# Second attention of a two-layer model: key-row scores from a second matmul, with the row maxima subtracted inside it

## Chip, core and metric

The kernel runs on one core of one Trainium2 chip. The metric is device time in microseconds (us). A profiled execution of the same program gives the trace; its span runs from the first to the last instruction.

## What is computed

1024 tokens of width 512 (2 sequences of 512) pass through an attention, a gated feed-forward, a second attention and a routed low-rank layer; each is added to its input and normalized. The change lies in the second attention (32 query heads, 8 key/value heads, head size 16, so 4 query heads share a key head):

```
q, k = rope(x @ Wq), rope(x @ Wk);  v = x @ Wv
scores = q @ k.T / sqrt(16), causal mask
ctx = softmax(scores) @ v
out = x + ctx @ Wo, normalized
```

## The kernel before

Everything is written by hand for the five engines, with semaphores; each engine runs its list in order. Matrix products are made from high and low parts (three matmuls for one).

The second attention (`attention1`, line 1248) first projects 8 tiles of 128 tokens to queries, keys and values, rotates them (`rotate` on VectorE, `turn_rows` on GpSimd), and turns them so that head elements lie on partitions (`turn_part` on TensorE, `high_part` on ScalarE, `low_part` on VectorE).

Then it works in 16 *units* (2 sequences x 8 key heads) of 4 query heads, 64 *slots* `s` in all. For a unit SyncE copies with 12 DMAs (`load_stacks`, lines 1411 to 1429) the high and low parts of keys and queries into `k_stack` and `q_stack`, 96 rows, so that one matmul with 96 rows gives the full product; keys of head versions 0 and 1 stand in separate rows with zeros between. There are two stacks of each. SyncE waits before load `u` until the scores of unit `u - 2` are made (line 1440).

One slot, over four engines:

- `scores(s)` on TensorE (1867 to 1885): for each of 4 query tiles a matmul, queries x seen keys, 512, 384, 128 and 256 keys wide, into three PSUM banks `ps_s`; a bank is filled again when its maxima are taken.
- `maxima(s)` on VectorE (1653 to 1663): adds the mask, takes the row maximum, writes the masked scores (`a_probs`) and the maximum (`a_neg_max`).
- `exps(s)` on ScalarE (1473 to 1478): four exponentials with the maximum as bias.
- `turn(s)` on TensorE (1887 to 1900): ten 128x128 transposes of probabilities into three banks `ps_t`, so that keys lie on partitions.
- `copy_turned(s)`: VectorE copies the first bank to SBUF (1665 to 1669), ScalarE the two others (1480 to 1486): `f_pT`, a ring of 6 slots.
- once per unit, `apply` (1902 to 1925): values x turned probabilities, four heads in four column strips of the array, in two parts; a column of ones beside the values gives the row sums. `evacuate` on VectorE, `turn_output` on TensorE, `join` on VectorE (division by the sum) follow.

The order is a loop over slots in each engine's list: TensorE does `turn(s)`, a part of `apply` or `turn_output` of the unit before, and `scores(s + 3)`; VectorE `maxima(s + 2)` and `copy_turned(s)`; ScalarE `exps(s + 1)` and `copy_turned(s)`. SyncE's queue carries the stack loads and, between them, weights of later stages; GpSimd splits those weights. After the loop the output is turned in tiles of 128 tokens (`turn_out`, `high_out`, `low_out`) and multiplied with `Wo` (`project_out`), with normalization and the routed layer behind it.

Of the kernel before, what the change touches and what calls it, by code (L numbers as in the profile page):

```python
# [15 lines left out]
P = 128  # L16
# [1184 lines left out]
HIGHEST = 3e38  # L1201
# [3 lines left out]
PROBS_AT = {3: 0, 2: SEQ, 0: SEQ + 3 * P, 1: 2 * SEQ}  # L1205
ROW_TILES = (3, 2, 0, 1)
PIECES = 3


TURNED_AT = {0: (0, 0), 1: (1, 0), 3: (1, 3 * P), 2: (2, 0)}  # L1210
TURNED_WIDTH = (SEQ, SEQ, 2 * P)
KEY_TILES = (0, 1, 3, 2)
# [4 lines left out]
RING = 6  # L1217
VALUE_COLS = HD1 + 2
HEAD_ROWS = P // GROUP1
APPLY_KEYS = ((0, 3), (1, 2))  # L1220
# [3 lines left out]
AHEAD_SCORES, AHEAD_MAXIMA, AHEAD_EXPS = 3, 2, 1  # L1224
CONSTANTS = 3
# [4 lines left out]
PARTS_IN_LOOP = {0: 7, 1: 8, 2: 9}  # L1230
# [17 lines left out]
def attention1(nc, t, w_o, w_f1, lora_b_in, small_in, result, psum):  # L1248

    ctx = ExitStack()  # L1250
    with ctx:
# [17 lines left out]
        q_stack = sb("q_stack", [P, 2, 2, SEQ], F32R)  # L1269
        k_stack = sb("k_stack", [P, 2, 2, SEQ], F32R)  # L1270
# [19 lines left out]
        probs = sb("probs", [P, GROUP1, HEAD_PROBS])  # L1290

        pT = over("pT", [P, RING, HEAD_PROBS], xT_at)
        b_at = aligned(nc.sbuf_base)
        sb("b_place", [P, 2, D])
        oT_now = sb("oT_now", [P, SEQ])
        by_at = aligned(nc.sbuf_base)
        by_cos, by_sin = sb("by_cos", [P, D + KV1 * HD1]), sb("by_sin", [P, D + KV1 * HD1])
        neg_max = sb("neg_max", [P, GROUP1, SEQ_TILES])
# [6 lines left out]
        main_first = over("main_first", [P, 1, D], xT_at + 4 * RING * HEAD_PROBS)  # L1305
# [5 lines left out]
        small = sb("small", [P, sum(SMALL.values())])  # L1311
        low = sb("low", [P, TILES, LORA])
        h = sb("h", [P, TILES, GATE_H])
        hT = sb("hT", [P, 2, P])

# [31 lines left out]
        ps_s, ps_t, ps_o = psum[0:3], psum[3:6], psum[6:8]  # L1347
        ps_out, ps_y, ps_side = psum[0:2], psum[2:4], psum[6:8]
# [6 lines left out]
        pads_set = sem("pads_set")  # L1355
# [5 lines left out]
        scored, max_done, exp_done = sem("scored"), sem("max_done"), sem("exp_done")  # L1361
        pT_ready, pT_dve, pT_act = sem("pT_ready"), sem("pT_dve"), sem("pT_act")
# [33 lines left out]
        def row_probs(s, qt):  # L1396
            return probs[:, s % GROUP1, PROBS_AT[qt]:PROBS_AT[qt] + (qt + 1) * P]

# [7 lines left out]
        def _(sp):  # L1406
# [4 lines left out]
            def load_keys(u, version, arrived):  # L1411
                b, g = divmod(u, KV1)
                for part, source in enumerate((kT_hi, kT_lo, kT_hi)):
                    to = part * PAIR_ROWS + version * HD1
                    sp.dma_start(k_stack[to:to + HD1, u % 2, version, :].bitcast(F32),
                                 source[g * HD1:(g + 1) * HD1, b * SEQ:(b + 1) * SEQ].bitcast(F32)).then_inc(arrived, 16)

            def load_queries(u, pair, arrived):
                b, g = divmod(u, KV1)
                first = (g % 2) * GROUP_COLS + pair * PAIR_ROWS  # L1420
                for part, source in enumerate((qT_hi, qT_hi, qT_lo)):
                    sp.dma_start(q_stack[part * PAIR_ROWS:(part + 1) * PAIR_ROWS, u % 2, pair, :].bitcast(F32),
                                 source[first:first + PAIR_ROWS, g // 2, b * SEQ:(b + 1) * SEQ].bitcast(F32)).then_inc(arrived, 16)
# [9 lines left out]
            sp.wait_ge(pads_set, 1)  # L1433
# [25 lines left out]
        def _(act):  # L1459
# [13 lines left out]
            def exps(s):  # L1473
                h = s % GROUP1
                for qt in ROW_TILES:
                    act.wait_ge(max_done, SEQ_TILES * s + maxima_before(qt))
                    act.activation(row_probs(s, qt), row_probs(s, qt), ACT.Exp, bias=neg_max[:, h, qt:qt + 1],  # L1477
                                   scale=-1.0).then_inc(exp_done, 1)

            def copy_turned(s):  # L1480
                if s >= RING:
                    act.wait_ge(applied, 2 * ((s - RING) // GROUP1 + 1))
                for piece in (1, 2):
                    width, at = TURNED_WIDTH[piece], piece * SEQ
                    act.wait_ge(pT_ready, PIECES * s + piece + 1)
                    act.activation(pT[:, s % RING, at:at + width], ps_t[piece][:, 0:width], ACT.Copy).then_inc(pT_act, 1)

            for tile in range(TILES - 1):
                if tile < 2:
                    norm.high(act, TILES - 2 + tile)  # L1490
                if tile == 0:
                    act.wait_ge(pads_set, 2)
# [5 lines left out]
                if tile == TILES - 2:  # L1498
                    exps(0)
            for s in range(SLOTS1 + 2):  # L1500
                u, h = divmod(s, GROUP1)
                if s + AHEAD_EXPS < SLOTS1:
                    exps(s + AHEAD_EXPS)
                if s < SLOTS1:
                    copy_turned(s)
                if s == 0:
                    copy_values(TILES - 1)
                    act.wait_ge(v_done, TILES)
                if s in PARTS_IN_LOOP:
                    high_part(PARTS_IN_LOOP[s])  # L1510

            def high_out(tile):
                act.wait_ge(out_turned, tile + 1)
                act.activation(outT_hi[:, :, tile * P:(tile + 1) * P], out_bank(tile), ACT.Copy).then_inc(out_hi, 1)
# [21 lines left out]
            for tile in range(4):  # L1536
                high_out(tile)
# [5 lines left out]
            for tile in range(TILES):  # L1543
# [6 lines left out]
                if tile + 4 < TILES:  # L1550
                    high_out(tile + 4)
# [25 lines left out]
        def _(pool):  # L1577
# [7 lines left out]
            pool.memset(k_stack[:, :, :, :].bitcast(F32), 0.0).then_inc(pads_set, 1)  # L1585
            pool.memset(v_flat[:, :], 1.0).then_inc(pads_set, 1)
            def turn_rows(tile):
# [4 lines left out]
            for tile in range(TILES - 1):  # L1592
                turn_rows(tile)
            def raise_diagonal(k):
# [11 lines left out]

            turn_rows(TILES - 1)
            for s in range(2, SLOTS1):
                pool.wait_ge(pT_dve, s)
# [15 lines left out]
        def _(dve):  # L1625
            ahead.add_row(dve, rows, norm, TILES - 1)
# [26 lines left out]
            def maxima(s):  # L1653

                if s >= GROUP1:
                    dve.wait_ge(pT_ready, PIECES * (s - GROUP1 + 1))
                for qt in ROW_TILES:
# [3 lines left out]
                    dve.tensor_tensor_reduce(row_probs(s, qt), ps_s[bank][:, at:at + seen], mask[:, SEQ - seen:SEQ],  # L1661
                                             -SCALE1, HIGHEST, ALU.add, ALU.min,
                                             neg_max[:, s % GROUP1, qt:qt + 1]).then_inc(max_done, 1)

            def copy_turned(s):
                if s >= RING:
                    dve.wait_ge(applied, 2 * ((s - RING) // GROUP1 + 1))
                dve.wait_ge(pT_ready, PIECES * s + 1)
                dve.tensor_copy(pT[:, s % RING, 0:SEQ], ps_t[0][:, :]).then_inc(pT_dve, 1)  # L1669

            def evacuate(n):
                dve.wait_ge(applied, 2 * (n + 1))
                if n >= 1:
                    dve.wait_ge(o_turned, n)
                dve.tensor_copy(oT_now[:, :], ps_o[n % 2][:, :]).then_inc(o_read, 1)
# [23 lines left out]
            for s in range(SLOTS1 + 3):  # L1699
                if s % GROUP1 == 2 and s >= GROUP1:  # L1700
                    evacuate(s // GROUP1 - 1)
                if s + AHEAD_MAXIMA < SLOTS1:
                    maxima(s + AHEAD_MAXIMA)
                if s < SLOTS1:
                    copy_turned(s)
                if s in PARTS_IN_LOOP:
                    low_part(PARTS_IN_LOOP[s])
                if s % GROUP1 == 3 and GROUP1 <= s < SLOTS1:
                    join(s // GROUP1 - 1)
# [13 lines left out]

            def low_out(tile):
                at = slice(tile * P, (tile + 1) * P)
                dve.wait_ge(out_hi, tile + 1)
                dve.tensor_tensor(outT_lo[:, :, at], out_bank(tile), outT_hi[:, :, at].bitcast(F32),
                                  ALU.subtract).then_inc(out_lo, 1)
# [55 lines left out]
            low_out(0)  # L1784
            join(UNITS1 - 1)
            for tile in range(1, 4):
                low_out(tile)
            dve.wait_ge(main_in, 48)
            for tile in range(TILES):
                add_output(tile)  # L1790
                if tile >= 2:
# [3 lines left out]
                if tile + 4 < TILES:  # L1795
                    low_out(tile + 4)
# [51 lines left out]
        def _(pe):  # L1848
# [18 lines left out]
            def scores(s):  # L1867

                u, h = divmod(s, GROUP1)
                if s == 0:  # L1870
                    pe.wait_ge(first_stack_in, STACK_DMAS // 2)
                elif s == 1:
                    pe.wait_ge(stack_in[0], STACK_DMAS // 2)
                elif h == 0:
                    pe.wait_ge(stack_in[u % 2], (u // 2 + 1) * STACK_DMAS - (STACK_DMAS // 2 if u % 2 == 0 else 0))
                for piece, tiles in enumerate(((3,), (2, 0), (1,))):
# [272 lines left out]
```

## Time and profile before

| | |
|---|---|
| median of 3 runs | 1177.17 us (1176.73 to 1177.77) |
| span of the profiled execution | 1175.2 us |
| second attention's loop over 64 slots | about 910 to 1092 us of the span |
| first matmul of the output projection behind it | 1098.4 us |

The span is read stage by stage. In a row of a timeline stand the start, the duration, engine and line, operation, output <- input, and in brackets the idle time before it with what ended it; several like instructions are one row (x4). TensorE has two rows: PE for matmuls (their ends are modelled and overlap) and PEld for weight loads. SPq is SyncE's queue of DMA issues.

### The profile page before, as it was taken

The numbers are of one execution on the slowest core, as the hardware profiler recorded it, in microseconds if no ns is written. First come the engines' busy times: TensorE is split into PE (matmuls) and PEld (weight loads), VectorE is DVE, ScalarE is ACT, GpSimd is POOL, SyncE is SP. The second block draws the span as 40 slices with busy tenths as digits, with TensorE's granted clock in tenths as the row PEclk, the third lists the DMA queues.
The fourth block names the chain that finished last, engine by engine and source line by source line (L and its number), as shares of the span: only waits on it lengthen the run. The fifth ranks groups of instructions, "written<-read, shape, count | busy, mean of one in ns | idle before, by whom it ended". The sixth has DMA issues, their size and how long they took to land. (4 is left out here: it accounts for less than half of the span.)

```text
span 1175.2 us, 20479 instructions
## 1 busy us (share of the span) xinstructions
PE 1135.8 (97%) x6634; PEld 952.6 (81%) x6634; DVE 780.6 (66%) x2463; ACT 705.3 (60%) x1646; POOL 410.5 (35%) x342
## 2 busy tenths in 40 slices
PE   7899999999999999999999999999999899999997
PEld 6788888788888888888888778888888677777786
DVE  6866776667776667766677762223336899999775
ACT  6656665556665566666566544543112899999524
POOL 4654554255444445534443513334013210020200
PEclk9999999999999999999999999999999999999999
DMA  6011110111110100110100012222001223321001
GB/s 230 19 40 43 37 32 24 30 28 37 53 29 21 37 32 24 55 27 11 45 19 28 1 37 75 68 78 76 1 18 24 57 70 80 98 53 33 2 1 72
DMA packets 30364, 51.24 MB, mean 44 GB/s; under 512 B 5680, under 2 KB 6576, under 8 KB 30256
## 3 DMA queue, kind: packets, MB, share of 16 engines
q1 hardware_dynamic: 29680, 48.85, 14.7%
q8 instruction: 55, 0.90, 0.3%
q10 hardware_dynamic: 576, 1.05, 0.2%
q14 instruction: 53, 0.43, 0.1%
HBM read 38.35 MB, written 2.10 MB: 34 GB/s over the span
## 5 line engine op out<-in xcount | busy, mean ns | idle before, releaser
L487 POOL TENSOR_TENSOR turned<-turned,sin 128x512 f32<-128x512 f32 x73 | 94.4, 1293 | 310.3 <-ACT turned L347 310.3
L363 ACT ACTIVATE probs<-probs,neg_max 128x256 f32<-128x256 f32 (+1 forms) x256 | 119.8, 473 | 11.3 <-DVE neg_max L580 11.3
L1477 ACT ACTIVATE a_probs<-a_probs,a_neg_max 128x512 f32<-128x512 f32 (+3 forms) x256 | 122.6, 562 | 0.1
L1661 DVE CUSTOM_DVE_ANT_0 a_probs<-bank,a_mask 128x512 f32<-128x512 f32 (+3 forms) x256 | 109.8, 486 | 6.2 <-PE bank L1881 6.1
L490 POOL TENSOR_TENSOR turned<-turned,by_cos 128x512 f32<-128x512 f32 x73 | 101.1, 1385 | 5.7
L96 PE MATMUL bank<-wo_hi,oT_hi 128*128 128x512 f32 x256 | 100.3, 392 | 1.7 <-DVE oT_lo L643 1.7
L734 PE MATMUL bank<-xT_hi,wq_hi 128*128 128x512 f32 x256 | 101.7, 397 | 0.0
L734 PE MATMUL bank<-xT_lo,wq_hi 128*128 128x512 f32 x256 | 100.3, 392 | 0.0
L734 PE MATMUL bank<-xT_hi,wq_lo 128*128 128x512 f32 x256 | 100.0, 391 | 0.0
L96 PE MATMUL bank<-wo_hi,oT_lo 128*128 128x512 f32 x256 | 99.9, 390 | 0.0
L96 PE MATMUL bank<-wo_lo,oT_hi 128*128 128x512 f32 x256 | 99.7, 389 | 0.0
L426 ACT ACTIVATE oT_hi<-bank 128x512 fp32r<-128x512 f32 x64 | 38.2, 596 | 93.4 <-PE bank L96 93.4
L422 ACT ACTIVATE pT_hi<-bank 128x512 fp32r<-128x512 f32 x112 | 61.6, 595 | 52.0 <-PE bank L773 52.0
L638 DVE TENSOR_TENSOR pT_lo<-bank,pT_hi 128x512 fp32r<-128x512 f32 x112 | 72.8, 686 | 22.1 <-ACT pT_hi L422 16.5
L1899 PE MATMUL bank<-identity,a_probs 128*128 128x128 f32 x640 | 81.3, 274 | 5.0 <-DVE f_pT L1669 5.0
L576 DVE CUSTOM_DVE_ANT_0 probs<-bank,mask 128x256 f32<-128x256 f32 (+1 forms) x256 | 85.0, 386 | 0.0
L553 DVE TENSOR_TENSOR by_cos<-bank,cos 128x512 f32<-128x512 f32 x73 | 50.3, 689 | 49.4 <-ACT turned L347 49.3
L346 ACT ACTIVATE turned<-bank 64x512 f32<-64x512 f32 x73 | 43.5, 596 | 63.3 <-PE bank L734 62.7
L1899 PEld LDWEIGHTS bank<-identity,a_probs 128*128 128x128 f32 x640 | 70.0, 140 | 9.0 <-issue 7.6
L643 DVE TENSOR_TENSOR oT_lo<-bank,oT_hi 128x512 fp32r<-128x512 f32 x64 | 44.2, 691 | 48.9 <-ACT oT_hi L426 47.7
L762 PE MATMUL bank<-kT_hi,qT_hi 128*128 128x256 f32 (+1 forms) x256 | 76.0, 297 | 0.0
L592 DVE TENSOR_SCALAR probs<-probs,inv_sum 128x256 f32<-128x256 f32 (+1 forms) x240 | 72.0, 363 | 2.1
(234 smaller groups left out, 3155.1 us busy)
## 6 DMA issues: line engine op xcount, KB each, us to landing
staged<-weights SPq DMA_DIRECT2D x70, 256.0 KB, 2.7
f_staged<-weights_f SPq DMA_DIRECT2D x33, 256.0 KB, 2.7
a_q_stack<-a_qT_hi SPq DMA_DIRECT2D x64, 64.0 KB, 2.0
rows<-x_rows SPq DMA_DIRECT2D x2, 1024.0 KB, 7.4
a_k_stack<-a_kT_hi SPq DMA_DIRECT2D x64, 32.0 KB, 2.0
a_q_stack<-a_qT_lo SPq DMA_DIRECT2D x32, 64.0 KB, 2.0
out<-rows SPq DMA_DIRECT2D x8, 256.0 KB, 2.0
a_raw<-weights_qkv SPq DMA_DIRECT2D x4, 384.0 KB, 4.4
```

Of the source, the lines that this page charges most:

```text
L96: mm = pe.matmul(out, a, b, start=(n == 0), stop=(n == len(steps) - 1))
L363: act.activation(probs[:, s % 2, h, 0:width], probs[:, s % 2, h, 0:width], ACT.Exp, bias=neg_max[:, s % 2, h:h + 1], scale=SCALE0, accum_o ...
L487: pool.tensor_tensor(at, at, sin[:, :], ALU.mult).then_inc(sin_done, 1)
L490: pool.tensor_tensor(at, at, by_cos_at(a, first), ALU.add).then_inc(roped, 1)
L576: dve.tensor_tensor_reduce(probs[:, s % 2, h, 0:width], ps_s[h // 2][:, (h % 2) * 2 * P:(h % 2) * 2 * P + width], seen, 1.0, LOWEST, ALU.a ...
L592: dve.tensor_scalar(probs[:, s % 2, h, 0:width], probs[:, s % 2, h, 0:width], inv_sum[:, s % 2, h:h + 1], None, ALU.mult).then_inc(probs_d ...
L638: dve.tensor_tensor(pT_lo[:, kb, :], ps_t[kb][:, :], pT_hi[:, kb, :].bitcast(F32), ALU.subtract).then_inc(pT_lo_done, 1)
L734: mm = pe.matmul(ps_a[a % 2][:, :], w[hi][:, k, :], part[:, k, cols], start=(n == 0), stop=(n == 3 * KC - 1))
L762: mm = pe.matmul(ps_s[pair][:, (h % 2) * 2 * P:((h % 2) * 2 + count) * P], q[:, u % 2, h, at], k[:, u % 2, keys], start=(n == 0), stop=(n ...
L1477: act.activation(row_probs(s, qt), row_probs(s, qt), ACT.Exp, bias=neg_max[:, h, qt:qt + 1], scale=-1.0).then_inc(exp_done, 1)
L1661: dve.tensor_tensor_reduce(row_probs(s, qt), ps_s[bank][:, at:at + seen], mask[:, SEQ - seen:SEQ], -SCALE1, HIGHEST, ALU.add, ALU.min, neg ...
L1899: mm = pe.transpose(ps_t[piece][:, at:at + P], row_probs(s, qt)[:, kb * P:(kb + 1) * P], ident[:, :])
```

## The change

Scores are made twice. As before, query rows x keys, from which now only the maxima are kept: VectorE writes its masked scores as bfloat16 into a tile that nobody reads, and the maxima into columns of `tops`. Once per unit TensorE turns the 16 columns of maxima (`turn_tops`), ScalarE copies them negated into `top_rows` (`copy_tops`), and SyncE writes them with 2 DMAs (`load_tops`) into two spare rows of the query stack; GpSimd has set ones in those rows of the key stack. A second set of matmuls with 98 rows (`key_scores`) then gives keys x queries with the maximum already subtracted. ScalarE takes three exponentials straight from PSUM into `pT` (now a ring of 8), and GpSimd sets the part above the diagonal to zero (`prune`). The transposes and copies of probabilities are gone.

The maxima run 7 slots ahead (LEAD), with 4 stacks. The evacuation of a unit moves from VectorE to ScalarE, values are applied in three parts from one slot later, and the turning of the first four output tiles moves into slots 58 to 61; two units' outputs and the last unit's value matmuls move behind the first tiles of the output projection.

```
...
+STACKS = 4
+TOP_ROW = STACK
+STACK_ROWS = STACK + 2
+LEAD = 7
+RING, RING_IN_X = 8, 6
-APPLY_KEYS = ((0, 3), (1, 2))
+APPLY_KEYS = ((0,), (1,), (3, 2))
+APPLY_PARTS = len(APPLY_KEYS)
+APPLY_LAG = GROUP1 + 1
-AHEAD_SCORES, AHEAD_MAXIMA, AHEAD_EXPS = 3, 2, 1
+OUT_AHEAD = 58
...
```

On SyncE:

```
+            def load_tops(u):
+                sp.wait_ge(top_ready, u + 1)
+                for version in range(2):
+                    rows_of = slice(version * 2 * SEQ_TILES, (version + 1) * 2 * SEQ_TILES)
+                    to = q_stack[u % STACKS][TOP_ROW + version:TOP_ROW + version + 1, :, :].rearrange("a p (t c) -> a (p t) c", c=P)
+                    sp.dma_start(to.bitcast(F32), top_rows[rows_of, :].bitcast(F32)).then_inc(top_in[u % 2], 16)
+
+            sp.wait_ge(stack_set, 2 * STACKS)
             sp.wait_ge(part_lo, TURNS_OF[0])
             load_stacks(0)
             load_stacks(1)
-            for u in range(2, UNITS1):
-                if u == KV1:
-                    sp.wait_ge(part_lo, TURNS_OF[1])
-                sp.wait_ge(scored, PIECES * GROUP1 * (u - 1))
-                load_stacks(u)
+            for u in range(UNITS1):
+                load_tops(u)
+                if u + 2 < UNITS1:
+                    if u + 2 == KV1:
+                        sp.wait_ge(part_lo, TURNS_OF[1])
+                    if u >= 2:
+                        sp.wait_ge(keyed, PIECES * GROUP1 * (u - 1))
+                    load_stacks(u + 2)
...
```

On ScalarE:

```
             def exps(s):
                 if s >= RING:
+                    act.wait_ge(applied, APPLY_PARTS * ((s - RING) // GROUP1 + 1))
+                for piece, width in enumerate(KEY_WIDTH):
+                    act.wait_ge(keyed, PIECES * s + piece + 1)
+                    act.activation(pT(s)[:, piece * SEQ:piece * SEQ + width], ps_t[piece][:, 0:width], ACT.Exp,
+                                   scale=SCALE1).then_inc(exp_done, 1)
+
+            def copy_tops(u):
+                act.wait_ge(top_turned, u + 1)
+                act.activation(top_rows[0:4 * SEQ_TILES, :], ps_top[u][0:4 * SEQ_TILES, 0:P], ACT.Copy,
+                               scale=-1.0).then_inc(top_ready, 1)
...
+            for s in range(SLOTS1):
+                exps(s)
+                if s % GROUP1 == 1 and s + 3 < SLOTS1:
+                    copy_tops((s + 3) // GROUP1)
+                if s % GROUP1 == 3 and s >= GROUP1 + 3:
+                    evacuate((s - GROUP1 - 3) // GROUP1)
+                if OUT_AHEAD <= s < OUT_AHEAD + SEQ_TILES:
+                    high_out(s - OUT_AHEAD)
...
```

On GpSimd:

```
+            def pad_keys(n):
+
+                pool.memset(k_stack[n][:, :, :].bitcast(F32), 0.0).then_inc(stack_set, 1)
+                pool.wait_ge(stack_set, 2 * n + 1)
+                pool.affine_select(k_stack[n][:, :, :], k_stack[n][:, :, :], [[-1, 2], [0, SEQ]], ALU.not_equal, 1.0,
+                                   base=-TOP_ROW, channel_multiplier=1).then_inc(stack_set, 1)
...
             for tile in range(TILES - 1):
                 turn_rows(tile)
+                if tile < STACKS:
+                    pad_keys(tile)
...
+            def prune(s):
+
+                pool.wait_ge(exp_done, PIECES * (s + 1))
+                for first, step in ((0, SEQ), (SEQ + 3 * P, P)):
+                    pair = pT(s)[:, first:first + 2 * step].rearrange("p (a c) -> p a c", a=2)[:, :, 0:P]
+                    pool.affine_select(pair, pair, [[0, 2], [1, P]], ALU.is_ge, 0.0, base=0,
+                                       channel_multiplier=-1).then_inc(pruned, 1)
...
```

On VectorE, per slot:

```
+                    dve.tensor_tensor_reduce(unused[:, UNUSED_AT[qt]:UNUSED_AT[qt] + seen], ps_s[bank][:, at:at + seen], mask[:, SEQ - seen:SEQ],
+                                             1.0, LOWEST, ALU.add, ALU.max, top_column(s, qt)).then_inc(max_done, 1)
...
+            for s in range(SLOTS1):
+                if s % GROUP1 == 1 and s >= 2 * GROUP1 + 1:
+                    join((s - 2 * GROUP1 - 1) // GROUP1)
+                if s + LEAD < SLOTS1:
+                    maxima(s + LEAD)
+                if OUT_AHEAD <= s < OUT_AHEAD + SEQ_TILES:
+                    low_out(s - OUT_AHEAD)
...
```

On TensorE:

```
+            def key_scores(s, piece):
+
+                u, h = divmod(s, GROUP1)
+                if h == 0 and piece == 0:
+                    pe.wait_ge(top_in[u % 2], 32 * (u // 2 + 1))
+                if s >= 1:
+                    pe.wait_ge(exp_done, PIECES * (s - 1) + piece + 1)
+                for kb in KEY_PIECES[piece]:
+                    at = KEYS_AT[kb][1]
+                    mm = pe.matmul(ps_t[piece][:, at:at + SEQ - kb * P],
+                                   k_stack[u % STACKS][0:STACK_ROWS, h % 2, kb * P:(kb + 1) * P],
+                                   q_stack[u % STACKS][0:STACK_ROWS, h // 2, kb * P:SEQ], start=True, stop=True,
+                                   skip_group_check=True)
+                mm.then_inc(keyed, 1)
+
+            def turn_tops(u):
+                pe.wait_ge(max_done, SEQ_TILES * GROUP1 * (u + 1))
...
+                if u >= 3:
+                    pe.wait_ge(finished, u - 2)
+                pe.transpose(ps_top[u][:, 0:P], tops[:, u % 2, :], ident[:, :]).then_inc(top_turned, 1)
...
+            lead(2)
+            lead(3)
+            turn_part(PARTS_LAST[0])
+            lead(4)
+            turn_tops(0)
+            turn_part(PARTS_LAST[1])
+            lead(5)
+            turn_part(PARTS_LAST[2])
+            lead(6)
...
+            for s in range(SLOTS1):
+                for piece in range(PIECES):
+                    if s + LEAD < SLOTS1:
+                        scores(s + LEAD, piece)
+                    key_scores(s, piece)
+                if s % GROUP1 == 1 and s + 3 < SLOTS1:
+                    turn_tops((s + 3) // GROUP1)
+                if s >= APPLY_LAG and (s - APPLY_LAG) % GROUP1 < APPLY_PARTS:
+                    apply((s - APPLY_LAG) // GROUP1, (s - APPLY_LAG) % GROUP1)
+                if s % GROUP1 == 0 and s >= 2 * GROUP1:
+                    turn_output(s // GROUP1 - 2)
+                if s == OUT_AHEAD:
+                    pe.wait_ge(max_done, SEQ_TILES * SLOTS1)
+                if OUT_AHEAD <= s < OUT_AHEAD + SEQ_TILES:
+                    turn_out(s - OUT_AHEAD)
             for tile in range(TILES):
                 project_out(tile)
+                if tile == 0:
+                    turn_output(UNITS1 - 2)
+                    for part in range(APPLY_PARTS):
+                        apply(UNITS1 - 1, part)
+                if tile == 1:
+                    turn_output(UNITS1 - 1)
...
```

The scores keep their wait for the stack: the first of a unit's score matmuls waits until all 12 loads of that unit have landed (line 1875 before, unchanged in the new `scores`).

## Rows read from the trace of the kernel before

**Rows 1.** Windows: busy us (instructions) of each engine, TensorE's clock, DMA share, GB/s.
```profile
950.00:1080.00 130.00, 126.57 (x1090) 95.78 (x1088) 121.76 (x460) 123.08 (x284) 8.61 (x16) 1.00 0.27 67
```

**Rows 2.** Timeline of two heads in the steady loop.
```profile
986.11 0.71 PEld L1881 LDWEIGHTS bank<-a_k_stack,a_q_stack 96*128 96x128 f32 x4 [0.20 <-issue]
986.11 0.91 PE L1881 MATMUL bank<-a_k_stack,a_q_stack 96*128 96x512 f32 x4
986.76 0.69 DVE L1661 CUSTOM_DVE_ANT_0 a_probs<-bank,a_mask 128x512 f32<-128x512 f32 x1 [0.35 <-PE bank L1881]
986.76 1.12 PEld L1899 LDWEIGHTS bank<-identity,a_probs 128*128 128x128 f32 x10
...
987.99 0.87 ACT L1486 ACTIVATE f_pT<-bank 128x512 f32<-128x512 f32 x2
988.04 0.16 PEld L1920 LDWEIGHTS bank<-f_pT,a_v_tok 128*32 128x32 f32 x8 [0.17 <-issue]
...
988.41 0.69 DVE L1669 COPY f_pT<-bank 128x512 f32<-128x512 f32 x1
...
988.75 1.91 ACT L1477 ACTIVATE a_probs<-a_probs,a_neg_max 128x512 f32<-128x512 f32 x4
...
989.26 0.71 PEld L1881 LDWEIGHTS bank<-a_k_stack,a_q_stack 96*128 96x128 f32 x4 [0.41 <-issue]
...
993.49 0.47 PEld L1932 LDWEIGHTS bank<-identity,a_oT_now 128*128 128x128 f32 x4
```

**Rows 3.** Timeline of SyncE's queue: stack loads of three units.
```profile
987.11 0.51 SPq L1415 DMA_DIRECT2D a_k_stack<-a_kT_hi  x1
987.66 0.59 SPq L1415 DMA_DIRECT2D a_k_stack<-a_kT_lo  x1
...
993.98 0.59 SPq L1422 DMA_DIRECT2D a_q_stack<-a_qT_lo  x1
...
999.27 0.82 SPq L1415 DMA_DIRECT2D a_k_stack<-a_kT_hi  x1
...
1009.11 0.51 SPq L1415 DMA_DIRECT2D a_k_stack<-a_kT_hi  x1
```

**Rows 4.** The page's DMA issues: count, KB each, median us from issue to landing.
```profile
a_q_stack<-a_qT_lo SPq DMA_DIRECT2D x32, 64.0 KB, 2.0
```

**Rows 5.** Groups on ScalarE, 800 to 1092 us: count | busy us, mean ns | idle before.
```profile
L1486 ACT ACTIVATE f_pT<-bank 128x256 f32<-128x256 f32 x64 | 24.4, 382 | 0.0
...
L1464 ACT ACTIVATE a_v_tok<-bank 128x128 f32<-128x128 f32 x8 | 2.2, 280 | 21.6 <-DVE a_by_sin L1644 21.5
...
L1060 ACT ACTIVATE f_gated<-bank 128x512 f32<-128x512 f32 x2 | 1.2, 598 | 2.9 <-PE bank L96 2.9
```

**Rows 6.** Groups on GpSimd, 500 to 1092 us.
```profile
L518 POOL TENSOR_SCALAR probs<-probs,inv_sum 128x256 f32<-128x256 f32 x12 | 10.9, 923 | 9.3 <-DVE inv_sum L585 9.3
...
L1602 POOL CAST a_w_hi<-f_side_raw 128x256 fp32r<-128x256 f32 x4 | 1.6, 396 | 89.3 <-DVE f_pT L1669 89.3
```

**Rows 7.** Timeline of GpSimd in the projections of the second attention.
```profile
880.31 0.46 POOL L1590 TENSOR_TENSOR a_k_tok<-a_by_cos,a_by_sin 128x128 f32<-128x128 f32 x1
883.61 1.29 POOL L1589 TENSOR_TENSOR a_q_tok<-a_by_cos,a_by_sin 128x512 f32<-128x512 f32 x1 [2.84 <-DVE a_by_sin L1644]
```

**Rows 8.** Timeline of VectorE: the third head's first maximum.
```profile
914.36 0.68 DVE L1661 CUSTOM_DVE_ANT_0 a_probs<-bank,a_mask 128x512 f32<-128x512 f32 x1
```

**Rows 9.** Timeline of TensorE: first matmul of the output projection.
```profile
1098.38 0.48 PE L96 MATMUL bank<-a_w_hi,a_qT_hi 128*128 128x512 f32 x1
```

**Rows 10.** Timeline of TensorE: two early matmuls, and the last of all.
```profile
11.47 0.63 PE L734 MATMUL bank<-xT_hi,wk_lo 128*128 128x512 f32 x1
11.90 0.63 PE L734 MATMUL bank<-xT_hi,wq_hi 128*128 128x512 f32 x1
...
1169.57 0.40 PE L2018 MATMUL bank<-f_b_hi,f_low_T_lo 128*128 128x512 f32 x1
```

**Rows 11.** Windows: the granted clock (after the five engines) behind the last matmul.
```profile
1173.00:1174.00 1.00, 0.00 (x0) 0.00 (x0) 0.00 (x0) 0.00 (x0) 0.00 (x0) 0.51 1.02 381
```

More of the change, by code:

```diff
@@ L1347, in attention1 @@
         ps_s, ps_t, ps_o = psum[0:3], psum[3:6], psum[6:8]
+        ps_top = [psum[5]] + [ps_o[(u + 1) % 2] for u in range(1, UNITS1)]
         ps_out, ps_y, ps_side = psum[0:2], psum[2:4], psum[6:8]
@@ L1360, in attention1 @@
         stack_in = [sem(f"stack_in{n}") for n in range(2)]
-        scored, max_done, exp_done = sem("scored"), sem("max_done"), sem("exp_done")
-        pT_ready, pT_dve, pT_act = sem("pT_ready"), sem("pT_dve"), sem("pT_act")
+        scored, max_done = sem("scored"), sem("max_done")
+        top_turned, top_ready = sem("top_turned"), sem("top_ready")
+        top_in = [sem(f"top_in{n}") for n in range(2)]
+        keyed, exp_done, pruned = sem("keyed"), sem("exp_done"), sem("pruned")
         applied, o_read, o_turned = sem("applied"), sem("o_read"), sem("o_turned")
@@ L1497, in _ @@
                     act.wait_ge(v_done, SEQ_TILES)
[L1498 to L1514, printed above, removed]
+            copy_values(TILES - 1)
+            act.wait_ge(v_done, TILES)
+            high_part(PARTS_LAST[0])
+            copy_tops(0)
+            high_part(PARTS_LAST[1])
+            high_part(PARTS_LAST[2])
+            for s in range(SLOTS1):
[6 more added lines that the diff above has]
+                    high_out(s - OUT_AHEAD)
             def low_rows(tile):
@@ L1625, in _ @@
         def _(dve):
+            dve.memset(tops[:, :, :], 0.0)
             ahead.add_row(dve, rows, norm, TILES - 1)
@@ L1698, in _, with low_out @@
             rotate(TILES - 1)
[L1699 to L1709, printed above, removed]
+            maxima(2)
+            maxima(3)
+            low_part(PARTS_LAST[0])
+            maxima(4)
+            low_part(PARTS_LAST[1])
+            maxima(5)
+            low_part(PARTS_LAST[2])
+            maxima(6)
+            def low_out(tile):
+                at = slice(tile * P, (tile + 1) * P)
+                dve.wait_ge(out_hi, tile + 1)
+                dve.tensor_tensor(outT_lo[:, :, at], out_bank(tile), outT_hi[:, :, at].bitcast(F32),
+                                  ALU.subtract).then_inc(out_lo, 1)
+            for s in range(SLOTS1):
[5 more added lines that the diff above has]
+                    low_out(s - OUT_AHEAD)
             steps = [0]
@@ L1782, in choose @@
                                   ALU.add).then_inc(choice_done, 1)
[L1784 to L1787, printed above, removed]
             dve.wait_ge(main_in, 48)
@@ L1790, in _ @@
                 add_output(tile)
+                if tile < 2:
+                    join(UNITS1 - 2 + tile)
                 if tile >= 2:
@@ L1887, in turn @@
[L1887 to L1900 removed]
+                tiles = SCORE_PIECES[piece]
@@ L1956, in _, with lead @@
                     pe.wait_ge(norm.lo_done, TILES)
[L1957 to L1971 removed]
+                    for piece in range(PIECES):
+                        scores(0, piece)
+            def lead(s):
+                for piece in range(PIECES):
+                    scores(s, piece)
+            lead(2)
[7 more added lines that the diff above has]
+            lead(6)
             def turn_out(tile):
```

211 lines of the change are left out of this document (84 added, 127 removed).

## The prediction

> **What bounds the kernel now.** I read the windows first, then the timeline of two heads, then SyncE's own queue. In the stretch where the loop over the 64 heads of the second attention runs steadily, ScalarE is busy 123 of 130 us, VectorE 122, and GpSimd 9 [rows 1]. Per head ScalarE does four exponentials and two copies out of PSUM, back to back [rows 2]; TensorE does four score matmuls (they hold it 0.65 us, 986.11 to 986.76), ten transposes and a part of the value matmuls (1.22 us, 988.04 to 989.26) [rows 2]. The two SyncE issues at 987.11 and 1009.11 start loads two units apart: a unit of four heads takes 11.0 us, a head 2.75 [rows 3]. Now the queue that nobody waits for today: SyncE issues the 12 stack loads of a unit 0.63 us apart, from 987.11 to 993.98, and is done with them 3.5 us before the next unit; the loads land 2.0 us after their issue [rows 3, 4].
>
> **The change, part by part.** All times below are on the span of the profiled execution, 1175.2 us; the median of the runs is 1177.17, so 2.0 us lie around the span and are taken as unchanged.
>
> *ScalarE, per head.* Four exponentials and two copies go (about 2.6 us of work); three exponentials that read PSUM come, 512, 512 and 256 wide. No exponential of before reads PSUM; the nearest row is the Silu that does, 0.598 us for 512, and the 256-wide copy, 0.382 [rows 5]. The copies start the next instruction about 0.1 us before their own end (987.99 to 988.75 for two that end after 0.87) [rows 2], so 1.25 us per head. ScalarE stops being the bound.
>
> *VectorE, per head.* The four maxima stay: 986.76 to 988.41, 1.65 us [rows 2]; their output becomes bfloat16, which I cost at nothing, since each element is still read from PSUM. The 512-wide copy (0.69) goes, and the one per unit moves to ScalarE. About 1.8 us per head with the join.
>
> *TensorE, per head.* Ten transposes go (issued over 1.12 us), four key-row matmuls of the same widths as the scores come: 0.65. With a quarter of the value matmuls (two parts of 1.22) and of the output transposes (0.47) [rows 2]: 0.65 + 0.65 + 0.61 + 0.12 = 2.0 us.
>
> *GpSimd.* Two triangular selects of 256 elements a head are new, an operation with no row. The nearest are the 256-wide cast, 0.396, and the 256-wide multiply by a column, 0.923 [rows 6]; I take 0.6 and keep both ends. Even at 0.92 it is 7.4 us per unit, with two splits of a weight added under 10. The four pads of the key stacks (about 2 to 3.5 us each, from the same rows by width) lie in GpSimd's idle time of 2.8 us per tile and the slack behind it [rows 7], and load_stacks(0) comes a tile later: nothing.
>
> By these four alone a unit would take some 8.5 us and the loop would gain.
>
> *SyncE and the new wait.* Here I see the loss. SyncE is served in order. load_tops(u) waits for top_ready(u+1), and load_stacks(u+2) stands **behind it on the queue**. The scores of unit u+2 begin in TensorE's slot 4u+1 and wait for all 12 of those loads. In that same slot, after those scores, stands turn_tops(u+1), which makes the next tops: TensorE cannot turn the tops of u+1 before the stack of u+2 has landed, and SyncE doesn't load that stack before the tops of u. That is a ring, closed once per unit:
> - 14 issues on SyncE: the first gap 0.55, then 12 of 0.63: the last issue starts 8.1 us after the first; it lands 2.0 later [rows 3, 4]: 10.1. In five units of 15 an issue is held longer (one of them 0.82 for 0.59 [rows 3]); a mean of 0.2 us: 10.3.
> - Landing to the next top: a hand-over of 0.15 (a first score matmul's end to VectorE's start in rows 2, an estimate), eight matmuls 1.30 and 0.26 until the last is out (0.91 less 0.65) [rows 2], hand-over 0.15, ScalarE's third exponential 0.38, the copy of the tops 0.28 [rows 5], hand-over to SyncE 0.1: 2.6.
>
> Sum 12.9 us per unit against 11.0 now, with TensorE idle about 4 us in each. What waits behind TensorE's wait at scores(4u+8): the keys, the value matmuls, so ScalarE and GpSimd; VectorE runs dry. The waits for keyed (two units old) and for top_in (two slots after the issue) end earlier.
>
> *Start.* VectorE's third head starts at 914.36 as now [rows 8]; two heads of maxima, the last scores of lead(4), the transpose and the copy make the first tops at 918.6. The ring runs 14 times (u = 0 to 13 load a stack): tops of unit 14 at 918.6 + 14 x 12.9 = 1099.2, slot 53 of TensorE ended 0.7 before, at 1098.5.
>
> *End.* No load is left to wait for. Slots 54 to 57: matmuls 1.30 each (0.65 in the last) plus value parts by columns (1.22 for 640 is 0.97 for 512, 0.73 for 384): 7.6 us. Slots 58 to 63: ScalarE 6 x 1.25, four splits of the output and two evacuations of 0.5: 10.5, with handing over 11.5. project_out(0) starts at 1117.6 instead of 1098.4 [rows 9]: 19.2 later, although the turning of four tiles (7 us between the loop and 1098.4 today) is now in the loop. Behind it TensorE gets two output transposes and one unit's value matmuls, 2 x 0.47 + 2.43 = 3.4, and about 0.5 of waiting. In all + 23.1: a span of 1198.3, **a time of 1200.3**.
>
> **The clock, weighed.** In the first us of the kernel, after an idle start, 512-column matmuls follow each other at 0.43 us, which is the half level; after the last matmul (1169.57, done at 1169.97) the granted clock is 0.51 from 1173 on, that is 1.2 of 2.4 GHz [rows 10, 11]. So an idle time of 3 us was once enough, and the ring leaves TensorE idle for about 4 us per unit. The Trainium skill (TensorE: Matmul & The Clock Gate, HAM oscillation — how this bites in real kernels) speaks against the change here: an engine that waits for a DMA between groups of matmuls falls back to half rate and begins every group slow. By that rule the ring grows as in the second case below; by the row, which is one case at the very end, it may or may not.
>
> **The rivals.**
> - *Ring, full clock* (the forecast): 1200. For it: every term but the hand-overs has a row. Ends: with no lengthened issue and 0.3 less handing over the ring is 12.4, so 1193, and 1190 with a tight end; at 13.3 it is 1206, with a loose end 1209.
> - *Ring and a clock that falls in each wait.* The eight matmuls (2560 columns) then take 2560 x 0.43/512 = 2.15 instead of 1.30 and the last result comes later: about + 1.0 us per ring, 14 x 1.0: **1214**. The rest of a unit's matmuls have the 4 us of idle time to be slow in. It decides from the unit on in which the wait is long enough for the clock.
> - *Faster: the ring doesn't close*, because the 14 issues follow each other faster than rows 3 show. Place: SyncE's queue; price: a unit of 9.1 us (14 x 0.63 and a wait), so 1200.3 - 14 x 3.8 = **1147**. The point from which it decides: a ring below 11.0, which needs issues 0.48 apart. All issues of rows 3 stand against it, and the loads themselves are the same.
> - *GpSimd becomes the bound*: from 1.6 us per select (8 in a unit make 12.9). At 2.0 it would be 16 us per unit, **1243**. Both rows of rows 6 are far below.
>
> That the transposes would stay is no case: the function that makes them is gone.
>
> **How the numbers follow.** Ring 0.72, ring with the clock falling 0.14, not closing 0.08, GpSimd 0.06. Time 1200.3. The range 1190 to 1217 takes in the ends of the ring and the falling clock and leaves out the last two and the far tails. A measurement of this kernel tells 0.2% (2.4 us) from no change: slower 0.91, faster 0.08, same 0.01.
>
> **What would show it.** In SyncE's queue: groups of 14 issues, 12.9 us from group to group, and load_tops waiting on ScalarE's copy of the tops for about 4 us each time. TensorE's largest wait: the score matmul on the DMA of the query stack, 14 times, 3 to 4.5 us. ScalarE and VectorE busy 50 to 65% of the loop, three exponentials of about 0.6, 0.6 and 0.38. The select near 0.4 to 0.9. If score matmuls hardly wait for DMA and units follow in 9 us, the ring argument is wrong; if TensorE's clock is below 1 in the loop, the second case holds; if applies wait for GpSimd, the last.

## The result, and the profile after

The changed kernel takes **1215.36 us** (median of 4 runs, 1211.18 to 1218.12) against 1176.95 for the kernel before: ratio 1.0319, interval 1.0294 to 1.0343. Forecast: 1200.3, range 1190 to 1217. The profiled execution, the longest of the four, took 1218.1 with a span of 1216.3. Below it is read in the order of the prediction.

Windows of the kernel after: the lead-in of the loop, the stretch of [rows 1], and ten us at the loop's end (columns as in [rows 1]).

```profile
920.00:930.00 10.00, 6.76 (x22) 5.33 (x21) 6.91 (x30) 3.99 (x6) 0.77 (x2) 0.50 0.26 60
950.00:1080.00 130.00, 103.51 (x667) 68.74 (x665) 73.87 (x330) 60.94 (x135) 34.74 (x88) 0.84 0.26 65
1115.00:1125.00 10.00, 10.00 (x54) 7.49 (x51) 4.50 (x18) 5.11 (x11) 1.92 (x6) 0.58 0.00 0
```

ScalarE fell from 123 to 61 of 130 us and VectorE from 122 to 74, so both have stopped being the bound. Yet the loop is slower, and TensorE's clock, 1.00 in [rows 1], is 0.84 here, 0.50 in the lead-in and 0.58 at the end, where TensorE is busy all the time.

SyncE's queue after, two rings: one tops pair (L1461, x2), the loads behind it, the next tops pair.

```profile
959.26 1.38 SPq L1461 DMA_DIRECT2D f_q_stack<-f_top_rows  x2
960.68 0.78 SPq L1438 DMA_DIRECT2D a_k_stack<-a_kT_hi  x1
...
967.82 0.59 SPq L1445 DMA_DIRECT2D a_q_stack<-a_qT_lo  x1
...
973.18 1.38 SPq L1461 DMA_DIRECT2D a_q_stack<-f_top_rows  x2
...
1001.34 1.38 SPq L1461 DMA_DIRECT2D a_q_stack<-f_top_rows  x2
1002.83 0.56 SPq L1438 DMA_DIRECT2D a_k_stack<-a_kT_hi  x1
...
1009.76 0.59 SPq L1445 DMA_DIRECT2D a_q_stack<-a_qT_lo  x1
1014.12 1.38 SPq L1461 DMA_DIRECT2D f_q_stack<-f_top_rows  x2
```

Where [rows 3] had groups of 12 issues every 11.0 us, there are groups of 14, here 13.92 and 12.78 us apart. In all, 14 rings run from 919.09 to 1110.14: 13.65 us each, forecast 12.9.

TensorE in the same two rings: the score matmuls behind the landing, up to the matmul that turns the tops (L1958).

```profile
969.87 0.80 PE L1926 MATMUL bank<-a_k_stack,a_q_stack 96*128 96x512 f32 x1 [3.83 <-DMA a_q_stack<-a_qT_lo]
970.46 0.63 PE L1941 MATMUL bank<-f_q_stack,f_k_stack 98*128 98x512 f32 x1
...
972.38 0.41 PE L1958 MATMUL bank<-identity,f_tops 128*128 128x128 f32 x1
...
1011.79 0.49 PE L1926 MATMUL bank<-a_k_stack,a_q_stack 96*128 96x512 f32 x1 [1.99 <-DMA a_q_stack<-a_qT_lo]
1012.12 0.40 PE L1941 MATMUL bank<-a_q_stack,a_k_stack 98*128 98x512 f32 x1
...
1013.17 0.27 PE L1958 MATMUL bank<-identity,f_tops 128*128 128x128 f32 x1
```

The wait for the stack is there, with the releaser that the prediction named. In the first ring the matmuls run at half rate and the next tops pair is issued 3.31 us after the first score matmul; in the second, at full rate, 2.33. Eight of the 14 rings are of the first kind. The two kinds nearly alternate. Five times a unit that began at full rate was followed by a wait for the stack, of 3.59 to 4.33 us, that ended at half rate. A unit that began at half rate fills more of its ring with its slower matmuls: six of eight such were followed by one at full rate.

Groups of the kernel after, 910 to 1110 us (count | busy us, mean ns | idle before): the new operations.

```profile
L1511 ACT ACTIVATE f_pT<-bank 128x512 f32<-128x512 f32 x84 | 47.0, 595 | 75.3 <-PE bank L1941 74.1
L1511 ACT ACTIVATE f_pT<-bank 128x256 f32<-128x256 f32 x42 | 16.4, 389 | 0.0
L1516 ACT ACTIVATE f_top_rows<-bank 16x128 fp32r<-16x128 f32 x15 | 3.8, 250 | 0.7 <-PE bank L1958 0.7
...
L1659 POOL TENSOR_SCALAR_AFFINE_SELECT f_pT<-f_pT 128x256 f32<-128x256 f32 x82 | 31.4, 406 | 103.2 <-ACT f_pT L1511 103.2
...
L1715 DVE CUSTOM_DVE_ANT_0 a_unused<-bank,a_mask 128x512 bf16<-128x512 f32 x60 | 41.4, 690 | 77.1 <-PE bank L1926 77.1
```

The exponentials cost what the Silu of [rows 5] does, the select what the cast of [rows 6] does, and the maxima with bfloat16 output what they did in [rows 2]. The idle times show who waits: ScalarE and VectorE for TensorE, GpSimd for ScalarE.

The first matmul of the output projection in the kernel after, for [rows 9]:

```profile
1136.27 0.50 PE L96 MATMUL bank<-a_w_hi,a_qT_hi 128*128 128x512 f32 x1
```

### The profile page after: what moved, and what is told of

Read it like the earlier page. It is cut to its first block and busy times, and to the rows that moved or that the text cites. A ratio compares the mean times of both kernels' runs of the same rounds, so it can differ in the third digit from the quotient of the medians.

```text
span 1216.3 us, 19482 instructions
## 1 busy us (share of the span) xinstructions
PE 1146.2 (94%) x6266; PEld 947.1 (78%) x6266; DVE 736.9 (61%) x2384; ACT 638.7 (53%) x1486; POOL 464.2 (38%) x477
## 5 line engine op out<-in xcount | busy, mean ns | idle before, releaser
L1715 DVE CUSTOM_DVE_ANT_0 a_unused<-bank,a_mask 128x512 bf16<-128x512 f32 (+3 forms) x256 | 113.2, 488 | 86.9 <-PE bank L1926 85.3
L1511 ACT ACTIVATE f_pT<-bank 128x512 f32<-128x512 f32 x144 | 67.6, 531 | 77.9 <-PE bank L1941 76.7
L1926 PE MATMUL bank<-a_k_stack,a_q_stack 96*128 96x512 f32 x192 | 69.6, 418 | 29.9 <-DMA a_q_stack<-a_qT_lo 26.5
L1926 PEld LDWEIGHTS bank<-a_k_stack,a_q_stack 96*128 96x128 f32 x192 | 45.2, 240 | 61.4 <-DMA a_q_stack<-a_qT_lo 29.5
L1659 POOL TENSOR_SCALAR_AFFINE_SELECT f_pT<-f_pT 128x256 f32<-128x256 f32 x96 | 36.7, 406 | 117.1 <-ACT f_pT L1511 117.1
```

What stands on the lines that cost most here:

```text
L1511: act.activation(pT(s)[:, piece * SEQ:piece * SEQ + width], ps_t[piece][:, 0:width], ACT.Exp, scale=SCALE1).then_inc(exp_done, 1)
L1715: dve.tensor_tensor_reduce(unused[:, UNUSED_AT[qt]:UNUSED_AT[qt] + seen], ps_s[bank][:, at:at + seen], mask[:, SEQ - seen:SEQ], 1.0, LOWES ...
L1926: mm = pe.matmul(ps_s[piece][:, at:at + (qt + 1) * P], q_stack[u % STACKS][0:STACK, h // 2, qt * P:(qt + 1) * P], k_stack[u % STACKS][0:ST ...
```

## The experiments

All are edits of the changed kernel, each timed beside the kernel before (medians 1176.7 to 1178.0 us). In the short diffs `at` stands for the unchanged access patterns.

**e1: the tops leave SyncE's queue.** ScalarE issues them itself, right behind its copy; SyncE has only loads, and each stack a semaphore of its own.

```
...
             for u in range(UNITS1):
-                load_tops(u)
...
             def copy_tops(u):
                 act.activation(top_rows[...], ps_top[u][...], ACT.Copy, scale=-1.0).then_inc(top_ready, 1)
+                act.wait_ge(top_ready, u + 1)
+                for version in range(2):
...
+                    act.dma_start(at, top_rows[rows_of, :]).then_inc(top_in[u % 2], 16)
```

> The two DMAs of the tops are issued by ScalarE behind its copy of them; SyncE's queue carries the 12 stack loads of a unit alone (a semaphore per stack). Ring theory: no load stands behind the tops any more, so stacks are loaded as early as the keys of two units before allow; a unit takes 8.7 to 9.3 us by TensorE's own work, the score matmul waits hardly at all for DMA, TensorE's clock stays at 1.0, and the time falls by 14 x 4.5 to about 1148 (1140 to 1160). Rival (the second set of matmuls, the exponentials out of PSUM or GpSimd's select are what makes the kernel slow, and the order of SyncE's queue does not matter): still over 1200, with waits for ScalarE or GpSimd.

Measured: **1152.34 us**, ratio 0.9791 (0.9775 to 0.9808). The same DMAs, the same bytes, another queue: 63 us less than the changed kernel, and faster than the kernel before. One window and two waits (us in total, times, longest) of e1, 950 to 1060 us:

```profile
950.00:1060.00 110.00, 108.24 (x845) 74.49 (x838) 88.41 (x406) 74.98 (x172) 47.64 (x118) 1.00 0.32 81
```

```profile
PEld bank L1923 <- DVE f_tops L1712: 22.5, 36, 0.8
...
PEld bank L1923 <- DMA a_q_stack<-a_qT_lo: 1.1, 1, 1.1
```

TensorE is busy 108 of 110 us at full clock, the wait for the stack has come down to 1.1 us, and units follow mostly 8.85 us apart. The weight loads of its score matmuls wait 22.5 us in all for VectorE's maxima, largely beneath matmuls still under way, so how much of the 8.85 is TensorE's own work is not settled. The prediction's 8.5 us for a unit without the ring was near; the place of two DMAs is worth the 63 us.

**e2: half of the loads ahead of the tops' wait**, all still on SyncE, with a semaphore per stack as in e1.

```
-                load_tops(u)
                 if u + 2 < UNITS1:
...
-                    load_stacks(u + 2)
+                    load_stacks(u + 2, (0,))
+                load_tops(u)
+                if u + 2 < UNITS1:
+                    load_stacks(u + 2, (1,))
```

> SyncE issues 6 of the 12 stack loads before it waits for the tops, 6 behind them (a semaphore per stack); nothing is moved to another queue. Ring theory: 6 issues leave the ring, 3.8 us of the 12.9 at full clock and of the 13.7 measured; a unit takes 9.9 us (SyncE's own 14 issues need 9.1), the clock is mostly 1.0, and the time is about 1158 (1150 to 1170). Rival (SyncE's order does not matter): no change from 1215.

Measured: **1165.84 us**, ratio 0.9895 (0.9879 to 0.9912). It isn't ScalarE's queue that helps but six issues fewer in the ring; the tops pairs come 9.0 us apart where nothing else disturbs, 10.35 on average.

**e3: TensorE kept busy in its wait**, by 28 matmuls that nobody reads, ahead of the score matmul that waits.

```
+                if s % GROUP1 == 1 and s + LEAD < SLOTS1:
+                    pe.wait_ge(exp_done, PIECES * s)
+                    for _ in range(28):
+                        pe.matmul(psum[5][:, SEQ // 2:SEQ], kT_hi[:, 0:P], kT_hi[:, 0:SEQ // 2], ...)
```

> The ring as it is; before the wait for a stack TensorE makes 28 matmuls of 256 columns that nobody reads (about 3.4 us at full clock), so that it is busy in most of the wait. Theory that the clock falls in the wait and lengthens the ring: granted clock 1.0 in the loop, ring 12.9 to 13.1, time 1200 to 1205. Rival (the 13.7 us come from other terms, such as the longer issues of the tops and the hand-overs, and the clock costs nothing): 1212 to 1220, the ring as long as before.

Measured: **1214.42 us** (1212.30 to 1223.65), ratio 1.0335: a miss. TensorE's timeline in e3 says why:

```profile
971.71 0.50 PE L1926 MATMUL bank<-a_k_stack,a_q_stack 96*128 96x512 f32 x1 [0.87 <-DMA a_q_stack<-a_qT_lo]
...
975.31 1.94 PE L1978 MATMUL bank<-f_pT,a_v_tok 128*32 128x512 f32 x8 [1.95 <-POOL f_pT L1659]
977.18 0.80 PE L1926 MATMUL bank<-a_k_stack,a_q_stack 96*128 96x512 f32 x1
...
987.75 3.60 PE L2083 MATMUL bank<-a_kT_hi 128*128 128x256 f32 x28 [0.56 <-ACT f_pT L1511]
```

The first row is what was wanted: full rate behind the landing, and the next tops pair 2.34 us later, as in the undisturbed ring above. But then TensorE waits 1.95 us for GpSimd's selects, runs at half rate for some 9 us, comes to the unread matmuls after the stack has landed, and now these hold it up: that ring took 19.4 us and another 15.5. GpSimd was late because it had stood 9.8 us for a weight's DMA (8.9 in the kernel after), with the selects behind: SyncE issues that weight only behind the 12 loads of a unit. So e3, which cured the clock in most rings and made two others longer, does not tell what the clock costs.

**e5: the same, mended.** 14 unread matmuls per unit instead of 28, 32 in the lead-in, and GpSimd's splits of the second weights eight slots later.

```
-OUT_SLOTS = (2, 3, 4, 5, 10, 11, 12, 13)
+OUT_SLOTS = (2, 3, 4, 5, 18, 19, 20, 21)
...
+            busy(psum[4], 10)
             lead(3)
...
+                    busy(psum[5], 14)
```

> The changed kernel with SyncE's queue and the ring untouched, but TensorE kept from standing idle: fewer unread matmuls than in e3 (14 of 256 columns, about 1.7 us at the full clock, at the start of the slot that waits for the stack, and 32 in the lead-in, where the clock first fell), and GpSimd's second set of weight splits eight slots later, so that the triangular selects do not queue behind its 8.9 us wait for the weights. Theory (ring, lengthened by the half clock): from the landing to the next tops issue the changed kernel took 3.31 us in a ring at half clock (969.87 to 973.18) and e3 took 2.34 in rings at full clock (971.71 to 974.05); with 8.56 from the first to the last issue and 2.05 of landing that is a ring of 12.95 us at full clock against 13.65 measured on average, and an end of about 20 us from the fifteenth tops to the output projection instead of 26. 14 x 0.7 + 6 = 16 us less than 1215: 1200, between 1196 and 1206, with the granted clock at 0.95 or more in nine windows of ten. Rival (the ring is 13.6 us for another reason, the clock only shows in work that has time): 1212 to 1218 with a clock of 1.0.

Measured: **1207.44 us** (1206.16 to 1209.14), ratio 1.0255 (1.0238 to 1.0272): above the 1196 to 1206 expected. The two edits together gain 8 us, not 16. Its 14 rings take 187.4 us, against 191.05: five still lost the clock (3.4 us in all), and single loads were held longer at issue, 5.0 us in all where the kernel after had 2.7, as this one of SyncE's queue in e5:

```profile
990.62 1.51 SPq L1438 DMA_DIRECT2D f_k_stack<-a_kT_hi  x1
```

What holds such an issue is open: the kernel before shows it too [rows 3], and in the stretches looked at no engine's row goes with it. The four undisturbed rings of e5 took 12.71 to 12.79. From the fifteenth tops to the output projection e5 took 20.5 us, the kernel after 26.1. e5 too changes two things: the ring that begins at 972.65 took 12.78, the same ring of the kernel after, with the selects late, 14.47, and that part of the gain may be the moved splits'.

**e6 and e7: the dose.** e6 issues four tops DMAs instead of two (the other two into rows that no matmul reads) and waits for all; e7 makes one of the two.

```
-                for version in range(2):
+                for version in range(4):
...
```

```
+                to = q_stack[u % STACKS][TOP_ROW:TOP_ROW + 2, :, :].rearrange("a p (t c) -> a (p t) c", c=P)
+                sp.dma_start(to.bitcast(F32), top_rows[0:4 * SEQ_TILES, :].bitcast(F32)).then_inc(top_in[u % 2], 16)
...
```

> The changed kernel, but load_tops issues four DMAs instead of two: the same 16 rows once more into two rows of the query stack that no matmul reads, and the key scores wait for all four. Nothing else is changed. Theory (SyncE's issues are in the ring): each ring gets two more issues of 0.69 us, the spacing of the two tops DMAs in the changed kernel, so + 1.38 us per ring and + 19 us in 14 rings: 1234, between 1228 and 1240, with groups of tops issues 15.0 us apart instead of 13.65. Rival (the loads are waited for, but TensorE or another engine sets the pace, as its 94% busy share suggests): 1213 to 1219.

> The opposite step: the two DMAs of the tops as one DMA of 16 rows into both rows of the stack; the output is the same. Theory (issues are in the ring): one issue of 0.69 us fewer in each of 14 rings: - 9.7 us, 1205.6, between 1199 and 1211, tops issues about 12.95 us apart. If the one DMA takes longer to issue because it has twice the rows, less of that. Rival (pace set elsewhere): 1213 to 1218.

Measured: e6 **1231.92 us** (ratio 1.0474, 1.0450 to 1.0499), e7 **1204.94 us** (1.0227, 1.0207 to 1.0247). SyncE's queue in e6, and then in e7:

```profile
1009.72 2.71 SPq L1462 DMA_DIRECT2D a_q_stack<-f_top_rows  x4
...
1024.79 1.37 SPq L1462 DMA_DIRECT2D f_q_stack<-f_top_rows  x2
```

```profile
999.38 0.66 SPq L1459 DMA_DIRECT2D a_q_stack<-f_top_rows  x1
...
1012.39 0.66 SPq L1459 DMA_DIRECT2D f_q_stack<-f_top_rows  x1
```

Two issues more make the rings 14.97 us on average, 1.32 more than in the kernel after; one fewer makes them 13.01, 0.64 fewer, though one ring of e7 took 17.81 (GpSimd's wait for a weight, as in e3). Like for like it is clearer: rings at half rate without a long issue took 13.67 to 13.75 us in the kernel after, 15.01 to 15.12 in e6, 12.97 to 13.05 in e7. An issue of 0.66 to 0.69 us, the same for 8 rows and for 16, comes back in the ring almost whole, in both directions; a pace set by another engine would have left the rings as they were. The times as a whole, 10.4 us less and 16.6 more, hold something else besides: from the fifteenth tops to the output projection e6 took 21.8 us and e7 21.9, the kernel after 26.1.

**e4: the ring opened by the order of the slots.** The maxima run six slots ahead instead of seven, so that the matmul that turns the tops stands ahead of the scores that wait for the stack.

```
-LEAD = 7
+LEAD = 6
...
-            lead(6)
```

> The maxima run 6 slots ahead instead of 7, nothing else: the scores of unit u+2 then begin in slot 4u+2, behind the turning of the tops of u+1 instead of before it. Ring theory: two units of tops are under way at once, a ring of about 20 us closes over two units, a unit takes about 10.3 us with a wait of some 1 us for the maxima, and the time falls to about 1164 (1155 to 1180). Rival (what counts is the number of issues or the new work, not where the wait stands): 1210 or more; a shorter lead should then only cost.

Measured: **1188.78 us** (ten executions, 1178.87 to 1200.65; the ratio, 1.0075 with an interval of 1.0044 to 1.0107, is of the nine up to 1195.47): 27 us less than the changed kernel, as the ring would have it, but 25 more than expected. One row of TensorE's timeline, and one window of e4:

```profile
1003.45 0.33 PE L1957 MATMUL bank<-identity,f_tops 128*128 128x128 f32 x1 [1.32 <-DVE f_tops L1715]
```

```profile
930.00:950.00 20.00, 19.69 (x81) 13.93 (x81) 11.42 (x48) 9.57 (x20) 8.89 (x20) 0.50 0.26 60
```

The matmul that turns the tops now waits for the maxima of scores just made, 1.3 us per unit: units of 10.4 us where e1 has 8.85. And in some units TensorE runs at half clock though it hardly idles: 16.3, 16.2 and 15.2 us for a unit.

**e8 and e9: e1 with the lead-in filled.** Unread matmuls in TensorE's waits ahead of the loop, 32 in e8 and 44, placed otherwise, in e9, whose edit is shown.

```
             lead(2)
+            pe.wait_ge(part_lo, PARTS_AFTER[TILES - 2][0] + 1)
+            busy(psum[4], 12)
             lead(3)
             turn_part(PARTS_LAST[0])
+            busy(psum[4], 4)
             lead(4)
             turn_tops(0)
+            busy(psum[4], 6)
...
             lead(5)
+            busy(psum[4], 14)
...
             lead(6)
+            busy(psum[4], 8)
```

> e1 (tops issued by ScalarE, 1152.3 us) with 32 unread matmuls of 256 columns in the four waits of TensorE's lead-in. In e1 the granted clock was 0.57 from 920 to 930 us and 0.70 from 930 to 950, and the tops of the first units came 12.2, 9.6 and 10.2 us apart, where they are 8.85 apart later at full clock. Theory (the lead-in's waits let the clock fall, and TensorE is the bound of e1's loop): the first units close up by 3 to 6 us in all, 1148, between 1145 and 1151, with the clock at 0.95 or more from 920 to 950. Rival (the lead-in is paced by VectorE's maxima, so the clock buys nothing, and the unread matmuls hold up score matmuls that VectorE waits for): 1152 to 1156.

> e8 with its unread matmuls placed otherwise: 12, 4, 6, 14 and 8 of them instead of 10, 6, 6 and 10, none any longer ahead of the matmul that turns the first tops (in e8 the first tops issue came 0.94 us later than in e1, 919.28 against 918.34), and 8 in the last wait before the loop, 0.82 us long, behind which e8's profiled execution fell to half clock (matmuls of 0.80 and 0.63 us from 926.16 on). Theory (what is left of the half clock costs e8 its spread of 1145.8 to 1151.1): no half clock from 920 to 950 us, the first four tops issues about 9 to 10 us apart, 1146, between 1143 and 1148. Rival (the first units are paced by something else, the clock only follows): 1148 to 1151, with the first tops issues 11.7, 9.6 and 10.5 us apart as in e8.

Measured: e8 **1148.19 us** (1145.78 to 1151.10), ratio 0.9748 (0.9726 to 0.9770); e9 **1145.45 us** (1144.59 to 1146.08), ratio 0.9731 (0.9715 to 0.9747). The window of 930 to 950 us, in e1 and then in e9:

```profile
930.00:950.00 20.00, 20.00 (x109) 15.13 (x110) 14.49 (x63) 12.51 (x29) 10.41 (x24) 0.70 0.22 51
```

```profile
930.00:950.00 20.00, 19.27 (x143) 13.34 (x144) 16.39 (x78) 14.88 (x34) 11.06 (x26) 1.00 0.33 76
```

As busy, a third more matmuls. e8's time is in its range, but the clock that it was to keep at 0.95 or more was 0.80 from 920 to 930 us and 0.67 from 930 to 950 in its profiled execution, the longest of its four; in e9 it is 1.00 in both windows. e9 is the fastest version here: 31.5 us below the kernel before, 70 below the changed one.

## Why the forecast was right in its mechanism and 15 us short

The sum was made for the span, 1198.3; it came out at 1216.3. By its steps:

| step | forecast | measured | difference |
|---|---|---|---|
| first tops issue | 918.6 | 919.09 | + 0.5 |
| 14 rings | 180.6 | 191.05 | + 10.5 |
| last ring to output projection | 18.4 | 26.13 | + 7.7 |
| behind it | 80.7 | 80.03 | - 0.7 |

*The ring* is shown: e1, e2 and e4 take it apart in three ways and each gains 27 to 63 us; e6 and e7 scale it. Its size at full clock was right: the undisturbed rings of the kernel after took 12.69 to 12.79 us, and with the 2.7 us of longer issues spread over 14 that is 12.9. Inside it two terms were off against each other: the tops pair keeps SyncE 1.42 to 1.50 us, not 1.18 (each of the two DMAs, for which there was no row, takes it some 0.7, not 0.55 and 0.63), and the way from the first score matmul to the next issue is 2.33, not 2.45.

*The step that failed* is the weight given to the clock: "Ring, full clock (the forecast)" was put at 0.72 and "Ring and a clock that falls in each wait" at 0.14. In the kernel after, the first score matmul took 0.49 to 0.51 us behind five waits of 1.80 to 2.52 us, and 0.79 to 0.80 behind eight waits of 2.18 to 4.33, six of them over 3.5. Eight rings lost 0.98 us each (3.31 less 2.33), 7.8. In one more (14.47 us) TensorE, at half rate and held 0.75 us by GpSimd's selects, came 1.7 late to a stack that had landed. In another (13.40) the last load landed late: the first score matmul came 2.71 us after that issue, against 2.01 to 2.11 in the others that waited, so 0.7. Longer issues have 2.7. With 14 x 12.72 (8.93 for the issues, 1.45 to the first score matmul, 1.39 to the turning, 0.95 to the next issue) that makes 191.0. The row that should have decided was in the prediction, [rows 11]: the clock had fallen after 3 us of idleness, and the ring was to leave 4. The rule of the Trainium skill (TensorE: Matmul & The Clock Gate, HAM oscillation — how this bites in real kernels), that an engine which waits for a DMA between groups of matmuls starts each group slow, agrees with the ring of 969.87, where the wait was 3.83 us. The five rings behind waits of 1.80 to 2.52 us started at full rate. The ring that had the late landing:

```profile
1105.09 0.59 SPq L1445 DMA_DIRECT2D f_q_stack<-a_qT_lo  x1
...
1107.80 0.50 PE L1926 MATMUL bank<-f_k_stack,f_q_stack 96*128 96x512 f32 x1 [2.52 <-DMA f_q_stack<-a_qT_lo]
```

*The rival's number*, 1214, is nearly the time measured, by another sum: it has 14 slow rings where there were 8, and nothing at the end, where the half clock also counts. That it comes so near is luck, and the range held because it took this rival in. The end is the other part: 18.4 was summed with matmuls at full rate, and the window of 1115 to 1125 us shows 0.58 with TensorE busy throughout. e5, whose clock is 1.00 there, took 20.5: of the 7.7 us, 5.6 are put down to the clock and 2.1 to the sum itself. The end is not alike in all kernels, though: e6 and e7, in which nothing was done for the clock, took 21.8 and 21.9. By this ledger the clock has 7.8 + 5.6 and a part of the 1.7, of the 18.0 us that the profiled span was over the forecast (the median was 15.1 over). e5 is 7.9 us faster than the changed kernel, with the splits moved as well; it still loses 3.4 in its rings to the clock, and 2.3 more than the kernel after to issues held longer. So the ring is shown by runs of its own, and that a half clock costs time where TensorE is busy throughout is shown by e9 against e1; how the missing microseconds divide is read from one trace, not tried by a run of its own.

*The other rivals:* the ring closed, with issues 0.63 us apart as in [rows 3]; GpSimd is busy 35 of 130 us. *Right at no cost:* the maxima in bfloat16, the pads, the exponentials. *Right side, wrong value:* the select, 0.41 and not 0.6, nearest to the cast; it bounds nothing. *Missed:* GpSimd's splits wait for a weight that SyncE loads behind a unit's stack, 8.9 us, with the selects and so the value matmuls queued behind. The prediction counted the splits' work and not their wait:

```profile
971.48 0.40 POOL L1619 CAST a_w_hi<-a_staged 128x256 fp32r<-128x256 f32 x1 [8.93 <-DMA a_staged<-weights_o]
```

In e2, e3 and e7 TensorE stood 1.94 to 1.98 us for selects held up in this way, and the ring begun beside it was the longest of each: 15.54, 19.38 and 17.81 us.

## What to carry to other kernels

When a load is queued behind a wait on an engine that serves in order, follow what that load releases: if it leads back to the wait, the period is the sum round the ring, whatever the engines' busy shares say, and moving two DMAs per unit to another queue can be worth more than all work removed: here it saved 63 us, and with it the change as a whole gains some 25. Cost such a ring with TensorE at the clock that its own wait leaves it, and look at the stages at either end with the same eye. A busy share near 100% says little until the granted clock beside it has been read: 20 us of a busy TensorE held 109 matmuls at 0.70 in e1 and 143 at 1.00 in e9.

## What the runs showed that was not expected

A low clock outlasted the waits ahead of it: in e1 TensorE was busy 20.00 of 20 us from 930 to 950 with a granted clock of 0.70, in e4 19.69 of 20 at 0.50. These waits were short, 1.87 and 1.57 us in the lead-in of e1, with some work between. So 44 matmuls that nobody reads (28 such took 3.6 us in e3, so some 5.7 us of TensorE's time) made e9 6.9 us faster than e1 (5.9 with each taken against the kernel before that was timed beside it).
